# Two activation blocks on ScalarE each split in two, with table loads of their own, and a new timetable

## The reference, cut to what matters

```python
# layer 1: a selective-scan block, on layernorm(x)
h = x * rsqrt(mean(x * x) + EPS) * norm_scale
xs, res = split(h @ w_in, 2)                 # 512 channels each
res = silu(res)
xs = silu(conv4(xs))                         # causal, depthwise, 4 taps
delta, B, C = split(xs @ w_xproj, [16, 32])
delta = softplus(delta @ w_dt + b_dt)
state[t] = exp(delta * A) * state[t-1] + delta * xs * B      # 16 states per channel
out = (sum_n(state * C) + xs * D) * res
x = x + layernorm(layernorm(x) + out @ w_out)
# layer 2: two branches of 8 experts, on layernorm(x)
prod = (Q @ V) * cumsum(K @ W)
g = gelu(Q @ router_w1.T + b1)
weights = softmax(g @ router_w2.T + b2 + expert_bias)
out = (prod * weights) @ U + weights @ b, divided by the token's number
x = x + layernorm((fwd + alpha * inv) @ W_O.T)
```

## Time and profile before

| | |
|---|---|
| median of 3 runs | 2413.68 us (2412.34 to 2414.4) |
| the profiled execution, its own time | 2413.96 us |
| its span in the profile | 2412.2 us |
| granted clock of PE, mean | 0.941 |
| one period in the middle | about 140 us |

### The profile page before, as it was taken

How to read it: one execution, slowest core, us unless ns; L and a number is a source line. 1 busy time by engine, 2 the same in 40 slices (tenths; PEclk the granted TensorE clock), 3 DMA queues, 4 the chain that set the end, 5 groups by cost and what they waited for, 6 DMA issues and landing times.

```text
span 2412.2 us, 35956 instructions
## 1 busy us (share of the span) xinstructions
PE 2143.7 (89%) x9268; PEld 1300.3 (54%) x9268; DVE 2147.9 (89%) x2775; ACT 1839.0 (76%) x3893; POOL 1898.4 (79%) x1369
## 2 busy tenths in 40 slices
PE   5687899999998989899998999999898999998888
PEld 2455455564655556465655646565564656555454
DVE  2889999998999999999999989999999999999920
ACT  6675787869698787968778696978879797875644
POOL 1679797988889798888979888897988889796520
PEclk8796899898999989999999989999899999989899
DMA  6111101111111011111102011110211110011000
GB/s 135 36 45 39 45 32 32 58 31 54 37 57 33 27 61 30 54 36 58 33 27 62 30 52 37 58 36 23 64 32 54 36 58 31 26 51 35 27 9 9
DMA packets 83401, 101.70 MB, mean 42 GB/s; under 512 B 23480, under 2 KB 49872, under 8 KB 83168
## 3 DMA queue, kind: packets, MB, share of 16 engines
q1 hardware_dynamic: 83168, 99.06, 13.7%
HBM read 90.13 MB, written 8.91 MB: 41 GB/s over the span
## 4 chain that ended last, share of the span: by engine, by line
DVE 34%; issue 26%; PE 15%; ACT 13%; POOL 9%; DVEq 1%; ACTq 0%; POOLq 0%
DVE h L1425 15%; DVE yT L1441 11%; PE bank L827 7%; POOL bx L792 4%; PE stateT L1007 4%; ACT decay L1277 2%; DVE xs L1336 2%; PE bank L986 1%; DVE yT L1438 1%; POOL dx L718 1%; POOL delta L712 1%; ACT scratch L1207 1%; ACT res L1141 1%; ACT prodT L1064 1%; ACT o_rows L1045 1%
## 5 line engine op out<-in xcount | busy, mean ns | idle before, releaser
L792 POOL TENSOR_TENSOR bx<-dx,B_rows 128x1024 f32<-128x1024 f32 x512 | 1204.6, 2363 | 286.9 <-DVE h L1425 252.4
L1425 DVE TENSOR_TENSOR_SCAN h<-decay,bx 128x512 f32<-128x512 f32 x1024 | 1236.8, 1208 | 64.7 <-ACT decay L1277 51.9
L1277 ACT ACTIVATE decay<-delta,decay_rate 128x512 f32<-128x512 f32 x1024 | 702.4, 691 | 351.0 <-DVE h L1425 343.0
L1007 PE MATMUL stateT<-ident,h 128*128 128x128 f32 x4096 | 646.9, 291 | 176.2 <-DVE h L1425 119.3
L1007 PEld LDWEIGHTS stateT<-ident,h 128*128 128x128 f32 x4096 | 492.6, 148 | 523.4 <-issue 306.8
L1441 DVE SCALAR_TENSOR_TENSOR yT<-stateT,C_tok,yT 128x512 f32<-128x512 f32 x960 | 694.7, 724 | 47.7 <-PE stateT L1007 47.5
L827 PE MATMUL bank<-hT,w_in_sb 128*128 128x512 f32 x512 | 246.5, 611 | 23.5 <-DVE xs L1336 9.9
L827 PE MATMUL bank<-q_to_expert,xnT 128*128 128x512 f32 x512 | 261.5, 638 | 0.1
L827 PE MATMUL bank<-k_to_expert,cumT 128*128 128x512 f32 x512 | 258.4, 630 | 0.0
L986 PE MATMUL bank<-expert_to_out,prodT 128*128 128x256 f32 x1024 | 244.5, 382 | 6.4 <-issue 6.4
L1241 ACT ACTIVATE cum_sb<-bank,gate 128x64 f32<-128x64 f32 x1024 | 221.8, 326 | 22.9 <-PE bank L827 20.2
(11 more groups left out here) (164 smaller groups left out, 2584.8 us busy)
## 6 DMA issues: line engine op xcount, KB each, us to landing
B_rows<-B_scratch SPq DMA_DIRECT2D x256, 256.0 KB, 3.2
x_front<-in_L_attn_x SPq DMA_DIRECT2D x16, 512.0 KB, 5.3
x_back<-in_L_attn_x SPq DMA_DIRECT2D x16, 512.0 KB, 3.5
out<-x_back SPq DMA_DIRECT2D x16, 512.0 KB, 5.8
w_in_sb<-in_L_attn_w_in SPq DMA_DIRECT2D x1, 1024.0 KB, 5.9
cum_sb<-in_L_ffn_V_fwd SPq DMA_DIRECT2D x2, 256.0 KB
prod<-in_L_ffn_W_inv_exp SPq DMA_DIRECT2D x2, 256.0 KB
xnT<-in_L_ffn_W_fwd SPq DMA_DIRECT2D x2, 256.0 KB
```

The source lines that it names most:

```text
L792: pool.tensor_tensor(bx[use % BX_RING][:, :, :], dx[q.parity][:, 2 * half:2 * half + 2, :], row, ALU.mult).then_inc(s_bx.step(f"{n},{half} ...
L1007: last = pe.transpose(stateT[j % 2][:, c * P:(c + 1) * P], h[n % 2][:, c, j * P:(j + 1) * P], ident[:, :])
L1277: act.activation(decay[c % 2][:, :], delta[q.parity][:, c, :], ACT.Exp, scale=decay_rate[:, c, n:n + 1]).then_inc(s_exp.step(f"{n},{c}"), 1)
L1425: dve.tensor_tensor_scan(h[n % 2][:, c, :], decay[c % 2][:, :], bx[(2 * n + c // 2) % BX_RING][:, c % 2, :], 0.0, ALU.mult, ALU.add).then_ ...
```

## The change

The SiLU task becomes two, `silux` at beat 65 and `silur` at beat 121, each with a load of the SiLU table before and of the exp table behind. The Gelu task is run twice, at beats 76 and 81 of its period (332 and 337), over half of the columns each, and each with two table loads. The timetable is written anew: most tasks move by a few beats, some by more. Cut to the lines that the text speaks of:

```diff
 TIMETABLE = {
-    ("F", "x", "sp"): (89,),
-    ("F", "xs", "act"): (32, 36, 38, 43),
-    ("F", "tap", "act"): (None, 37, None, 45),
-    ("F", "cv", "pool"): (None, 45, None, 64),
-    ("F", "silu", "act"): (67,),
-    ("F", "proj", "act"): (83,),
+    ("F", "x", "sp"): (123,),
+    ("F", "xs", "act"): (35, 35, 39, 40),
+    ("F", "tap", "act"): (None, 35, None, 42),
+    ("F", "cv", "pool"): (None, 38, None, 63),
+    ("F", "silux", "act"): (65,),
+    ("F", "silur", "act"): (121,),
+    ("F", "proj", "act"): (82,),
...
-    ("F", "dt", "act"): (86, 90, 104, 108),
-    ("F", "ex", "act"): (88, 93, 105, 111),
-    ("F", "ln", "act"): (89, 96, 111, 115),
+    ("F", "dt", "act"): (87, 91, 104, 115),
+    ("F", "ex", "act"): (87, 92, 106, 117),
+    ("F", "ln", "act"): (89, 94, 108, 117),
...
-    ("B", "cum", "dve"): (323, 323),
-    ("B", "rt", "pe"): (324, 325, 327, 329),
-    ("B", "rt", "act"): (327, 329, 332, 333),
-    ("B", "gelu", "act"): (334,),
-    ("B", "logit", "pe"): (336,),
-    ("B", "logit", "act"): (340,),
-    ("B", "logit_rows", "pe"): (342,),
-    ("B", "lb", "dve"): (344,),
+    ("B", "cum", "dve"): (318, 319),
+    ("B", "rt", "pe"): (320, 325, 327, 328),
+    ("B", "rt", "act"): (323, 330, 331, 335),
+    ("B", "gelu", "act"): (332, 337),
+    ("B", "logit", "pe"): (338,),
+    ("B", "logit", "act"): (341,),
+    ("B", "logit_rows", "pe"): (339,),
+    ("B", "lb", "dve"): (340,),
...
-    ("L", "cum", "pe"): (346, 348, 366, 375, 383, 390, 403, 434),
-    ("L", "cum", "act"): (354, 358, 370, 376, 388, 392, 410, 438),
-    ("L", "pr", "dve"): (355, 368, 371, 384, 398, 430, 432, 438),
-    ("L", "t", "act"): (466,),
+    ("L", "cum", "pe"): (344, 348, 359, 375, 383, 390, 402, 432),
+    ("L", "cum", "act"): (355, 356, 368, 378, 391, 393, 409, 436),
+    ("L", "pr", "dve"): (364, 372, 374, 379, 398, 430, 432, 438),
+    ("L", "t", "act"): (467,),
 }
...
             def logit_task(b, k, use):
-                pe.wait_ge(b_act.sem, b_act.done(b, "gelu"))
+                pe.wait_ge(b_act.sem, b_act.done(b, "gelu1"))
...
-            def silu_task(b, k, use):
+            def silux_task(b, k, use):
                 if b.is_first:
-                    act.wait_ge(f_act.sem, f_act.done(b, "res3"))
-                    act.activation(res[b.parity][:, :, :], res[b.parity][:, :, :], ACT.Silu).then_inc(first_silu, 1)
                     act.preload_act_table_set(EXP_SET)
                     act.wait_ge(f_pe.sem, f_pe.done(b, "proj"))
-                    act.wait_ge(first_silu, 2)
+                    act.wait_ge(first_silu, 1)
                     act.sem_inc(f_act.step("silux"), 1)
-                    act.sem_inc(f_act.step("silur"), 1)
                     return
                 act.wait_ge(f_dve.sem, f_dve.done(b, "cvC2"))
                 act.wait_ge(f_pool.sem, f_pool.done(b, "cv33"))
                 act.sem_inc(passed["act"], 1)
                 act.preload_act_table_set("silu_and_others")
                 act.activation(xs[b.parity][:, :, :], xs[b.parity][:, :, :], ACT.Silu).then_inc(f_act.step("silux"), 1)
+                act.preload_act_table_set(EXP_SET)
+
+            def silur_task(b, k, use):
                 act.wait_ge(f_act.sem, f_act.done(b, "res3"))
+                act.sem_inc(passed["act"], 1)
+                act.preload_act_table_set("silu_and_others")
                 act.activation(res[b.parity][:, :, :], res[b.parity][:, :, :], ACT.Silu).then_inc(f_act.step("silur"), 1)
                 act.preload_act_table_set(EXP_SET)
...
             def gelu_task(b, k, use):
-                act.wait_ge(b_act.sem, b_act.done(b, "rt3"))
+                act.wait_ge(b_act.sem, b_act.done(b, f"rt{2 * k + 1}"))
                 act.sem_inc(passed["act"], 1)
                 act.preload_act_table_set("gelu_and_others")
-                act.activation(scratch[:, :, :], scratch[:, :, :], ACT.Gelu).then_inc(b_act.step("gelu"), 1)
+                act.activation(scratch[:, 2 * k:2 * k + 2, :], scratch[:, 2 * k:2 * k + 2, :], ACT.Gelu).then_inc(b_act.step(f"gelu{k}"), 1)
                 act.preload_act_table_set(EXP_SET)
```

More of the change, by code:

```diff
@@ L149 @@
-    ("B", "logit", "act"): (340,),
-    ("B", "logit_rows", "pe"): (342,),
-    ("B", "lb", "dve"): (344,),
-    ("B", "mx", "dve"): (345,),
-    ("B", "sub", "pool"): (354,),
+    ("B", "keep", "pool"): (258,),
+    ("F", "sum", "act"): (1,),
+    ("F", "sq", "act"): (10,),
+    ("F", "rs", "pool"): (19,),
+    ("F", "h", "act"): (19,),
+    ("F", "hT", "pe"): (21, 22),
+    ("F", "hT", "act"): (25, 29),
+    ("F", "x", "sp"): (123,),
+    ("F", "xs", "pe"): (30, 33, 36, 37),
+    ("F", "xs", "act"): (35, 35, 39, 40),
@@ new lines @@
+    ("F", "cvA", "dve"): (32, None, 37, None),
+    ("F", "cvB", "dve"): (33, None, 38, None),
+    ("F", "cvC", "dve"): (35, None, 39, None),
+    ("F", "tap", "act"): (None, 35, None, 42),
+    ("F", "cv", "pool"): (None, 38, None, 63),
+    ("F", "res", "pe"): (38, 42, 44, 54),
+    ("F", "res", "act"): (42, 44, 52, 61),
+    ("F", "silux", "act"): (65,),
+    ("F", "silur", "act"): (121,),
+    ("F", "proj", "pe"): (78,),
+    ("F", "proj", "act"): (82,),
+    ("F", "B", "sp"): (77,),
+    ("F", "Ct", "pe"): (117,),
@@ new lines @@
+    ("F", "Ct", "act"): (122,),
+    ("F", "dt", "pe"): (83, 87, 95, 110),
+    ("F", "dt", "act"): (87, 91, 104, 115),
+    ("F", "ex", "act"): (87, 92, 106, 117),
+    ("F", "ln", "act"): (89, 94, 108, 117),
+    ("F", "w", "pool"): (99, 109, 120, 122),
+    ("F", "w2", "pool"): (102, 113, 122, 124),
+    ("F", "d1", "pool"): (103, 116, 124, 124),
+    ("F", "row", "sp"): (126, 135, 139),
+    ("B", "y", "pe"): (263, 263, 264, 265),
+    ("B", "u", "dve"): (264, 264, 264, 267),
+    ("B", "o", "pool"): (272, 274, 275, 278),
@@ new lines @@
+    ("B", "wo", "pe"): (278, 280, 283, 289),
+    ("B", "r", "dve"): (283, 286, 290, 291),
+    ("B", "st", "dve"): (292,),
+    ("B", "ag", "dve"): (295,),
+    ("B", "rb", "pool"): (300,),
+    ("B", "t", "act"): (302,),
+    ("B", "x1", "pool"): (313,),
+    ("B", "st1", "dve"): (308,),
+    ("B", "ag1", "dve"): (309,),
+    ("B", "rb1", "pool"): (318,),
+    ("B", "xn", "act"): (315,),
+    ("B", "xnT", "pe"): (315, 317),
+    ("B", "xnT", "act"): (319, 320),
+    ("B", "cum", "dve"): (318, 319),
@@ L174 @@
-    ("L", "store", "sp"): (476,),
+    ("B", "gT", "pe"): (356,),
+    ("B", "gT", "act"): (367,),
+    ("L", "cum", "pe"): (344, 348, 359, 375, 383, 390, 402, 432),
+    ("L", "xv", "pe"): (355, 362, 372, 377, 397, 422, 430, 435),
+    ("L", "cum", "act"): (355, 356, 368, 378, 391, 393, 409, 436),
[4 rows of a table added]
+    ("L", "out", "act"): (390, 402, 446, 453),
+    ("L", "sq", "act"): (455,),
+    ("L", "rs", "pool"): (460,),
+    ("L", "t", "act"): (467,),
+    ("F", "dx", "pool"): (115, 121, 126, 130),
+    ("L", "x", "pool"): (476, 476),
@@ L175 @@
+    ("L", "store", "sp"): (475,),
 }
@@ L319, in program @@
                                                        "Ct": ["Ct"], "dt": ["dt{}"]}))
-        f_act = Steps(sem("f_act"), steps_of("act", "F", {"sum": numbered("sm"), "sq": numbered("sq"), "h": numbered("h"), "hT": ["hT{}"], "xs": ["cv{}"], "tap": ["tp{}1", "tp{}2", "tp{}3"], "res": ["res{}"], "silu": ["silux", "silur"],
+        f_act = Steps(sem("f_act"), steps_of("act", "F", {"sum": numbered("sm"), "sq": numbered("sq"), "h": numbered("h"), "hT": ["hT{}"], "xs": ["cv{}"], "tap": ["tp{}1", "tp{}2", "tp{}3"], "res": ["res{}"], "silux": ["silux"], "silur": ["silur"],
                                                           "proj": ["proj"], "Ct": ["Ct"], "dt": ["ab{}", "rl{}"], "ex": ["ex{}", "v{}"], "ln": ["ln{}", "u{}"]}))
@@ L330, in program @@
                                                        "logit": ["lg"], "logit_rows": ["lt"], "gT": ["gT"]}))
-        b_act = Steps(sem("b_act"), steps_of("act", "B", {"t": numbered("t"), "xn": numbered("xn"), "xnT": ["xnT{}"], "rt": ["rt{}"], "gelu": ["gelu"], "logit": ["lc"], "ex": ["ex"], "gT": ["gT"]}))
+        b_act = Steps(sem("b_act"), steps_of("act", "B", {"t": numbered("t"), "xn": numbered("xn"), "xnT": ["xnT{}"], "rt": ["rt{}"], "gelu": ["gelu{}"], "logit": ["lc"], "ex": ["ex"], "gT": ["gT"]}))
         b_dve = Steps(sem("b_dve"), steps_of("dve", "B", {"u": ["u{}"], "r": ["r{}"], "st": numbered("st"),
```

52 lines of the change are left out of this document (5 added, 47 removed), and 6 rows, old and new, of the table TIMETABLE.

## The result

The changed kernel takes 2429.55 us (median of 4 runs, 2429.05 to 2430.46) against 2414.04 us for the kernel before (4 runs): ratio 1.0068, interval 1.0053 to 1.0083. It is slower, as forecast, but by 15.5 us and not by 43.5. It lies in the wide range of 2424 to 2476 and outside the forecast's own 2448 to 2468.

A forecast was written before the change was run, and what follows sets the result against it. DVE was taken to bound the kernel, busy 133.3 of 139.8 us a period. Terms of -1.3, +2.4, +1.8 and -0.2 gave +2.7 us a period, +43.5 in all: 2458 us, range 2424 to 2476 (own range 2448 to 2468).

The forecast's parts named there:

- The measure of ACT's lateness: ACT may be 1.6 us late with a decay, plus DVE's other work in that window, before DVE waits.
- waits at 78, 82 and 84: DVE's waits for ACT around the two half Gelus and the centring: about 1.0, 2.0 and 1.3 us, 4.3 together.
- the small chain at 85: ACT's logit copy, PE's small transposes and DVE's bias addition, now closer together, delay PE's state transposes by 0.4 us.
- 2.76 us: Longest ACT block that fits without making DVE wait; half blocks of 4.5 (SiLU) and 3.76 us (Gelu) exceed it.
- Half a Gelu: Gelu over half its columns on ACT, estimated at 1.06 us by a line between two traced instructions.
- PE's waits at 94 and 107: DVE's waits of 1.24 and 1.14 us for PE, seen where PE's clock was 0.50; no change put in the sum.
- +1.8 for the second SiLU: Beats 116 to 124: the new SiLU block at 121 adds 1.8 us of waits a period, at 122 and 124.
- Rival 1: PE's clock recovers near beat 102 and the 1.14 us wait goes: 1.1 us a period less, 2442 us; chance 0.17.
- rival 2: A slow PE stretch near beat 88 every period, with its 1.24 us wait: up to 1.0 a period, 2473; chance 0.13.
- Beats 76 to 96: Half Gelus, centring, logit chain and dt pairs: waits of 5.0 us against 2.6 before, +2.4 us a period.
- The start: The first batch's second SiLU block stands on ACT ahead of the first decay: about 1.5 us late.
- beats 0 to 60: PE's and DVE's tasks move by a beat or two; DVE showed no wait there, so counted at nothing.

The follow-up runs named there:

- run 4: The kernel before, in its old timetable, with both the SiLUs and the Gelu split in two and nothing else changed; 2483.05 us, ratio 1.029.
- run 8: The changed kernel without the Gelus' four table loads, each half Gelu replaced by a copy of the same size; 2377.22 us, one run.
- run 1: The changed kernel's new timetable with the old blocks: both SiLUs joint at beat 65, the Gelu whole at 81; 2431.96 us, ratio to before 1.0079.
- run 2: The changed kernel with only the Gelu joined again, whole at beat 81, SiLUs still in two; 2407.75 us, ratio to before 0.9978.
- run 6: The changed kernel with the second SiLU block moved from beat 121 to 169, beat 41 of the next period; 2430.63 us, ratio to before 1.0073.
- run 11: New timetable, Gelu whole at beat 81, SiLUs split, second SiLU block moved from beat 121 to 169; 2415.17 us, ratio to before 1.001.
- run 9: The kernel before, old timetable, Gelu whole, only the SiLUs split, at beats 67 and 169; 2379.75 us, ratio 0.986.
- run 3: The changed kernel with both SiLUs joined again at beat 65, the Gelu still in two; 2452.64 us, ratio to before 1.0161.
- run 10: The kernel before, old timetable, Gelu whole, only the SiLUs split, at beats 67 and 121; 2432.38 us, ratio 1.0082.
- run 7: The changed kernel with the last dt matmul back at beat 102 and the third expert matmul group at 110; 2459.46 us, ratio to before 1.0192.

## Why the forecast was right in its sign and too high by 28 us

**The measure of ACT's lateness** was right. Its waits at 78, 82 and 84 were forecast as 1.0, 2.0 and 1.3 and measured as 0.94, 1.92 and 1.27; at 66 it was 0.15 against 0.32, at 121 to 124 1.8 against 1.54, and the small chain at 85 0.4 against 0.31. The blocks in the old table came out as counted too (run 4). A block that does not fit in 2.76 us made DVE wait, and run 8 shows the other side, where a block of about 1.07 us made none.

**Half a Gelu** was estimated at 1.06 us and takes 1.06. The four loads of 1.28 us around the Gelus cost 3.2 us a period (run 8), not their 5.1.

**The step that failed** is a term that had no line in the sum: PE's waits at 94 and 107 (in the rows they stand at beats 95 and 109) were left as they were, at a change of nothing, and +1.8 for the second SiLU was put on top. They were neither fixed nor separate. The later wait lost its 1.1 us at beat 109, and with the new table alone 0.99 stand at 121 and 123 (run 1), in the very place of the new block. Behind ACT's wait of 1.54 they can hardly be seen. So the block at 121 adds 0.5 us (runs 1 and 2), and removing it gives nothing (6, 11). The earlier wait grew by 0.7 and took more than half of this back. The prediction had the failure among its signs of being wrong ("if PE's waits at 94 and 107 change with the clock") and in rivals 1 and 2, but not in its sum.

This is not all of the 28 us. In the thirteen later periods the forecast is 16 us too high: 1.2 a period for PE's wait at 109, less 0.7 for the one at 91, and about 0.7 for the other terms together. The other 12 lie ahead of and behind these periods, as told below.

**The granted clock goes with PE's waits.** Within one kernel the order of the instructions is the same in every period, and the stretches at 0.50 (1.2 GHz) are not: in some periods one is missing, in others it lasts 3.4 us, in others 6.8. I sorted the ten middle periods of each trace by the stretch just ahead of a wait. DVE's wait in us, and in brackets the number of periods:

| wait, and in which kernels | no stretch | 3.4 us | 6.8 us |
|---|---|---|---|
| PE at 109; before and run 9 | 0 (4) | 0.21 to 0.22 (4) | 1.11 to 1.46 (12) |
| ACT at 112, same periods | 0.76 to 0.77 | 0.43 to 0.44 | 0 |
| PE at 95; before and run 9 | 0 (8) | 0 to 0.17 (4) | 1.19 to 1.45 (8) |
| PE at 91; the changed kernel and runs 1, 2, 3, 6, 11 | 0 (1) | 0.56 to 0.94 (27) | 1.18 to 1.82 (32) |
| PE at 123; runs 1, 3, 6, 11 | 0.44 (4) | 0.44 (3) | 1.15 where it begins at 112 (17), 0.45 to 1.15 where at 108 or 110 (16) |

So nearly all of PE's wait at 91, 95 and 109 comes and goes with the clock. At 123 about 0.44 us stands without any slow stretch and belongs to the new order of the tasks. No run sets the clock by itself; what stands here is that the waits follow it in every one of the periods counted.

The second line of the table is what the prediction could have seen: in the first of the two periods of the earlier trace rows, with a clock of 1.00, PE's wait is absent and one for ACT has come up in its place. Timeline of DVE in the kernel before, beat 112:

```profile
738.47 1.22 DVE L1425 TENSOR_TENSOR_SCAN h<-decay,bx 128x512 f32<-128x512 f32 x1 [0.77 <-ACT decay L1277]
```

And in run 9, where a stretch of 3.4 us stands ahead, both are there, beats 109 and 112:

```profile
1142.20 0.75 DVE L1447 SCALAR_TENSOR_TENSOR yT<-stateT,C_tok,yT 128x512 f32<-128x512 f32 x1 [0.22 <-PE stateT L1011]
1145.16 1.22 DVE L1431 TENSOR_TENSOR_SCAN h<-decay,bx 128x512 f32<-128x512 f32 x1 [0.43 <-ACT decay L1283]
```

In the changed kernel the same holds at the new block: in the four periods without a stretch near 112, ACT's waits at 122 and 124 are 1.64 together, with one they are less and PE's stand beside them. Run 3 shows PE's side alone, beats 121 and 123 behind a stretch that begins at 112, and beat 123 of the next period without one:

```profile
1037.40 0.75 DVE L1441 SCALAR_TENSOR_TENSOR yT<-stateT,C_tok,yT 128x512 f32<-128x512 f32 x1 [0.28 <-PE stateT L1007]
1040.43 0.75 DVE L1441 SCALAR_TENSOR_TENSOR yT<-stateT,C_tok,yT 128x512 f32<-128x512 f32 x1 [1.15 <-PE stateT L1007]
...
1182.27 0.75 DVE L1441 SCALAR_TENSOR_TENSOR yT<-stateT,C_tok,yT 128x512 f32<-128x512 f32 x1 [0.44 <-PE stateT L1007]
```

Rival 1, which took 1.1 us a period off and gave 2442, was half right. The stretch near 102 and the wait behind it did go, but a stretch at 108 to 112 took its place in six of ten periods, and a wait removed is not gained whole.

**Where the stretches fall.** In the kernel before they begin at beats 86 and 100 to 102, in the changed one at 84 to 86 and, in six of ten periods, at 108 to 112, and in runs 1, 2, 3, 6 and 11, all of the new table, at 84 to 86 and 108 to 112. In runs 4, 9 and 10 the later one stays at 100 to 104, as in the old table. In run 7, with two of PE's tasks put back, none begins at 110 to 112, and shorter ones of 3.4 us begin at 102 to 104 in three periods and at 114 to 116 in seven. So these tasks take part in where the stretches fall, though PE's wait at 109 did not return with them. What decides the place stays open.

**Beats 76 to 96** were forecast at +2.4; ACT's and the chain's part is +1.9. The 0.45 at beat 90 of before, which I kept as 0.3, is gone, and in its place stands PE's wait at 91, 1.35 where 0.64 had been at 95. That is +0.7 which belongs to rival 2: the standstill at 78 to 85 is followed by a stretch at 1.2 GHz in every period. But the length of the standstill is not what sets the wait: behind nearly the same standstill run 1 has 1.48 and run 2 has 0.81. In run 2 every stretch there lasts 3.4 us, in the changed kernel every other one 6.8. The windows of the changed kernel show PE busy for all of such a stretch:

```profile
992.00:998.80 6.80, 6.80 (x13) 3.12 (x14) 5.22 (x7) 6.74 (x13) 6.14 (x5) 0.50 0.50 163
```

**The ends and the first periods.** The start was forecast at +1.5 and is -1.9. In all kernels with the new table the first scan starts at 60.6 to 63.3 us, with the old one at 64.6 to 65.0. The first batch's extra block costs 0.8 to 1.9 of this gain (runs 1 and 2, run 3 and the changed kernel), near the 1.5 forecast. The table itself starts 3.5 us earlier, which I had not looked for. Behind the last first scan, +3.9 was forecast, 2.4 of it for the last Gelu, and +2.0 came. The first two periods were forecast at +3.0 and are -3.6. The largest item is one wait: DVE's at beat 19 of the first, behind PE, falls from 5.7 to 1.9 us. Others fall and rise (behind PE at beat 65 from 3.7 to 0.2, behind ACT at 122 from nothing to 2.0), and I did not take them apart. The prediction took beats 0 to 60 at nothing since DVE showed no wait there; the longest wait of the earlier trace rows, 5.7 us, stands at just this place. It lies in the long stretch at 0.50 of the start, which ends at 86.6 us before and at 80.6 after, and DVE goes on at 86.0 and at 81.1. What in the table ends it earlier stays open.

**The parts of the change**, from runs 1 and 2 and the changed kernel: the new timetable +2.0 us a period, the SiLUs' split -2.0, the Gelu's split +1.6. In the other order, by way of run 3, the Gelu's split is +1.3 and the SiLUs' -1.7, so the parts depend on each other. The forecast never took them apart, and did not see that the timetable costs as much as the whole change and that one of the three is a gain. The Trainium skill (ScalarE: Activation LUTs, "Table sets: the hidden batching unit") wants calls grouped by table set. That held here for the Gelu and not for the SiLU: in the kernel of run 9 two more loads a batch come with 1.4% less time, because where a block stands decides. The drain of 1380 ns that the same page of the Trainium skill adds to each load ("What ACT_TABLE_LOAD costs") does not appear in any of these traces: where the next instruction waits for nothing, it starts within 0.02 us of the load's end.

## What to carry to other kernels

An engine that works one or two tiles ahead of the bound engine has a fixed spare; compute it once (here 1.6 us, an estimate from the rows that came true to 0.3 us for most blocks), add the bound engine's other work in the window, and test each block against it. Where the block is too long, don't split it at the price of its overhead before asking whether half of it can stand where the bound engine is busy with something else.

Waits at one place don't add. Before a new wait is put into a sum, ask which wait of another engine already stands there or will be moved there, and before one is removed, which comes up behind it. Sort the periods of one trace by the granted clock first: the periods without a slow stretch show what lies beneath PE's wait.

## What was not expected of the hardware

- The stretches in which PE's clock was granted at 0.50 came at nearly the same beats in period after period, and moved when the timetable moved: the later ones lie at beats 100 to 108 before and mostly at 112 to 118 after.
- At beat 109 of the old table (before and run 9), a stretch of 3.4 us went with a wait of 0.2 us of DVE, and one of 6.8 us with 1.1 to 1.5.
- A 128x1024 Gelu took 1.06 us and a 128x2048 one 1.91, and every table load 1283 ns, with the next instruction starting 1.29 us after its start, where that one waited for nothing.
